# An eight-batch attention and feed-forward walk: the next batch's input norm made late in the walk, h in two halves, the cross-attention's exponential later

## The reference

```
x = x + cross_attention(layernorm(x), ctx)       # 16 heads of 64, 64 keys
n = layernorm(x)
dense:  q, k, v = n @ wq, n @ wk, n @ wv         # 16 heads of 16
        o = causal_softmax(q k / 4) v
        h = n + rmsnorm(o @ wo) * attn_norm_w
        d = h + rmsnorm(silu(h @ w1) * (h @ w3) @ w2) * ff_norm_w      # 1024 wide
sparse: top 2 of 8 experts by softmax(n @ router_w), each silu(n ew1) * (n ew3) @ ew2
        s = rmsnorm(weighted sum) * moe_norm_w
x = x + d + s
```

## Time and profile before

| | |
|---|---|
| median of 3 runs | 1732.98 us (1730.11 to 1733.04) |
| the profiled execution | 1727.69 us, its span 1725.6 us |
| mean granted clock of TensorE | 0.923 of full |
| busy PE, PEld, DVE, ACT, POOL | 83%, 55%, 48%, 32%, 31% |
| chain that ended last | PE 61%, DVE 13%, DMA 7%, POOL 6%, ACT 5%, SPq 4%, issue 4% |

### The profile page before, as it was taken

How to read it: one execution, slowest core, us unless ns; L and a number is a source line. 1 busy time by engine, 2 the same in 40 slices (tenths; PEclk the granted TensorE clock), 3 DMA queues, 4 the chain that set the end, 5 groups by cost and what they waited for, 6 DMA issues and landing times.

```text
span 1725.6 us, 23514 instructions
## 1 busy us (share of the span) xinstructions
PE 1435.5 (83%) x7689; PEld 945.7 (55%) x7690; DVE 834.7 (48%) x1733; ACT 551.2 (32%) x1178; POOL 533.1 (31%) x720
## 2 busy tenths in 40 slices
PE   7757998799879987998899879897988889999940
PEld 3533566556655665566556555664565365666620
DVE  0456435743664365446544644464347323333347
ACT  3230442154115402540343034304430513333322
POOL 3223215212422332233223331323142113555532
PEclk9985999999989998999899989998999889999975
DMA  5342007000600160025003400420050352222247
GB/s 216 126 101 59 2 4 156 14 1 19 141 14 1 37 123 14 1 64 97 13 1 89 72 13 1 115 45 14 1 123 13 44 156 65 88 85 85 85 165 255
DMA packets 107111, 117.18 MB, mean 68 GB/s; under 512 B 39416, under 2 KB 80912, under 8 KB 107024
## 3 DMA queue, kind: packets, MB, share of 16 engines
q1 hardware_dynamic: 88080, 98.10, 22.0%
q0 software_dynamic: 8576, 17.87, 3.3%
q10 hardware_dynamic: 10368, 0.04, 0.3%
HBM read 71.36 MB, written 44.21 MB: 67 GB/s over the span
## 4 chain that ended last, share of the span: by engine, by line
PE 61%; DVE 13%; DMA 7%; POOL 6%; ACT 5%; SPq 4%; issue 4%; ACTq 0%; POOLq 0%; DVEq 0%
PE ps L971 7%; PE ps L793 7%; PE ps L937 7%; PE ps L812 5%; DMA room<-parts_d 5%; DVE nm L1390 4%; PE ps L862 4%; PE ps L899 4%; PE ps L945 4%; PE ps L988 3%; PE ps L885 3%; SPq L501 3%; PE ps L826 2%; PE ps L782 2%; PE ps L919 2%
## 5 line engine op out<-in xcount | busy, mean ns | idle before, releaser
L1390 DVE TENSOR_REDUCE nm<-ps 128x2 f32<-128x256 f32 (+3 forms) x256 | 203.3, 821 | 139.2 <-PE ps L863 138.3
L1101 ACT ACTIVATE room<-ps 128x512 f32<-128x512 f32 x320 | 181.0, 598 | 152.4 <-PE ps L887 150.5
L937 PE MATMUL ps<-hT,w 128*128 128x512 f32 x768 | 213.5, 423 | 1.4 <-DVE hT L1418 1.4
L862 PE MATMUL ps<-room 96*128 96x128 bf16 (+3 forms) x512 | 135.5, 326 | 63.4 <-DMA room<-parts_d 43.3
L937 PEld LDWEIGHTS ps<-hT,w 128*128 128x128 f32 x768 | 145.3, 198 | 34.3 <-DVE hT L1418 3.3
L885 PE MATMUL ps<-room 99*128 99x384 bf16 (+3 forms) x512 | 132.2, 313 | 23.7 <-ACT room L1101 21.6
L1125 ACT ACTIVATE room<-ps 128x512 f32<-128x512 f32 x64 | 38.1, 596 | 343.3 <-PE ps L937 343.3
L971 PE MATMUL ps<-room 128*128 x288 | 137.4, 600 | 3.0 <-ACT room L1139 3.0
L945 PE MATMUL ps<-w,room 128*128 128x256 f32 x512 | 134.6, 393 | 0.0
L793 PE MATMUL ps<-room,xnT 128*128 128x512 f32 x256 | 133.0, 648 | 0.0
L1296 DVE TENSOR_TENSOR room<-ps,room 128x1024 f32<-128x1024 f32 x32 | 39.1, 1223 | 190.4 <-PE ps L793 190.4
(11 more groups left out here) (219 smaller groups left out, 2540.8 us busy)
## 6 DMA issues: line engine op xcount, KB each, us to landing
room<-parts_d SPq DMA_DIRECT2D x96, 256.0 KB, 6.7
room<-xs_d SPq DMA_DIRECT2D x72, 128.0 KB, 2.0
parts_d<-room SPq DMA_DIRECT2D x64, 128.0 KB, 1.8
room<-pair_d SPq DMA_DIRECT2D x8, 1024.0 KB, 7.7
room<-in_L_ffn_ew SPq DMA_DIRECT2D x24, 256.0 KB, 6.9
xin<-in_x SPq DMA_DIRECT2D x8, 512.0 KB, 11.8
parts_d<-xnT SPq DMA_DIRECT2D x32, 128.0 KB, 1.8
y_d<-hb SPq DMA_DIRECT2D x8, 512.0 KB, 2.6
```

The costliest lines, as they stand in the source:

```text
L862: mm(bank(o, n), q_rep[0:KREP, rep_at(h), t * P:n], k_rep[0:KREP, rep_at(h), 0:n], start=True, stop=False)
L937: last = mm(bank(up_banks(b, m)[i]), w[:, x, k, m * P:(m + 1) * P], hT[:, y, k, :], start=((x, y, k) == terms[0]), stop=((x, y, k) == term ...
L1101: done(fn(prob[:, u * 512:(u + 1) * 512], bank(6 + n % 2), ACT.Exp), "b_exp")
L1390: done(v.tensor_reduce(nm[:, t, 2 * hp:2 * hp + 2], pair_ps, AX.X, ALU.max, negate=True), "a_max")
```

## The change

- "x_stats" and "x_apply" leave `CROSS`; as "nx_stats" and "nx_apply" the same work is done for the next batch, behind "shift_parts" 0 in block 5 and at the end of block 6. Batch 0's stands at the head of walk 0, and walk 7 has none. POOL's root for it gets its own buffer and semaphore. "x_turn" comes after "m" 1 instead of after "m" 3 and "shift" 1.
- In the cross-attention "exp" 0 to 3 stand one or two PE steps later, and "sum" 1 between "cs" 2 0 and "cs" 2 1. PE's own order there stays as it was, but for "x_turn".
- "f_o_norm": POOL adds h in two halves of two tiles, each when its half of the scaled product is there; "f_h_turn" turns each half when it is ready.
- The net's first three blocks: gating on DVE ("fg" 0) comes before the second up product's step, and the routing steps and "slots" stand later.
- The maxima and sums of the cross-attention are counted by the general semaphore `dve_step`.
- The words of the change name replicating loads left with one queue; the kernel before has them all on SP's queue, and the diff touches no line of them.

```diff
 CROSS = [
-    ("x_stats",), ("m", 0), ("x_apply",), ("m", 1), ("m", 2), ("m", 3), ("shift", 1), ("x_turn",), ("bqk", 0), ("bqk", 1), ("f_hb",),
-    ("cs", 0, 0), ("cs", 0, 1), ("vw", 0), ("vw", 1), ("exp", 0), ("vw", 2), ("vw", 3), ("sum", 0), ("x_bias",),
-    ("cs", 1, 0), ("cs", 1, 1), ("exp", 1), ("sum", 1), ("ct", 0, 0), ("ct", 0, 1),
-    ("cs", 2, 0), ("cs", 2, 1), ("exp", 2), ("cv", 0, 0), ("cv", 0, 1), ("sum", 2), ("ct", 1, 0), ("ct", 1, 1),
-    ("cs", 3, 0), ("cs", 3, 1), ("exp", 3), ("cv", 1, 0), ("cv", 1, 1), ("sum", 3), ("ct", 2, 0), ("ct", 2, 1),
+    ("m", 0), ("m", 1), ("x_turn",), ("m", 2), ("m", 3), ("shift", 1), ("bqk", 0), ("bqk", 1), ("f_hb",),
+    ("cs", 0, 0), ("cs", 0, 1), ("vw", 0), ("vw", 1), ("vw", 2), ("exp", 0), ("vw", 3), ("sum", 0), ("x_bias",),
+    ("cs", 1, 0), ("cs", 1, 1), ("ct", 0, 0), ("ct", 0, 1), ("exp", 1),
+    ("cs", 2, 0), ("sum", 1), ("cs", 2, 1), ("cv", 0, 0), ("exp", 2), ("cv", 0, 1), ("sum", 2), ("ct", 1, 0), ("ct", 1, 1),
+    ("cs", 3, 0), ("cs", 3, 1), ("cv", 1, 0), ("exp", 3), ("cv", 1, 1), ("sum", 3), ("ct", 2, 0), ("ct", 2, 1),
...
-    ("v", 0), ("v", 1), ("f_h_turn",), ("v", 2), ("v", 3), ("route", 0), ("route", 1), ("fu", 0, 0), ("f_yb",), ("fu", 0, 1), ("fg", 0, 0), ("fg", 0, 1),
-    ("route", 2), ("fu", 1, 0), ("fu", 1, 1), ("fg", 1, 0), ("fg", 1, 1), ("fd", 0, 0), ("fd", 0, 1), ("slots",),
-    ("fu", 2, 0), ("fu", 2, 1), ("fg", 2, 0), ("fg", 2, 1), ("scatter",), ("fd", 1, 0), ("fd", 1, 1),
+    ("v", 0), ("v", 1), ("f_h_turn",), ("v", 2), ("v", 3), ("route", 0), ("fu", 0, 0), ("f_yb",), ("fg", 0, 0), ("fu", 0, 1), ("fg", 0, 1),
+    ("route", 1), ("fu", 1, 0), ("fg", 1, 0), ("fu", 1, 1), ("fg", 1, 1), ("route", 2), ("fd", 0, 0), ("fd", 0, 1),
+    ("fu", 2, 0), ("fg", 2, 0), ("fu", 2, 1), ("fg", 2, 1), ("slots",), ("scatter",), ("fd", 1, 0), ("fd", 1, 1),
...
-    STEPS += [("shift_parts", 0)] if _m == 5 else []
+    STEPS += {5: [("shift_parts", 0), ("nx_stats",)], 6: [("nx_apply",)]}.get(_m, [])
...
                     elif step[0] == "f_o_norm":
-                        need(pool, c, "wo_n", 2)
                         need(pool, c, "hb", 1)
-                        done(g.tensor_tensor(hb[:, :, :], hb[:, :, :], o_tok[:, :, :], ALU.add), "h")
+                        for i in range(2):
+                            need(pool, c, "wo_n", i + 1)
+                            done(g.tensor_tensor(hb[:, 2 * i:2 * i + 2, :], hb[:, 2 * i:2 * i + 2, :], o_tok[:, 2 * i:2 * i + 2, :], ALU.add), "h")
...
-                        turn(c, hb, (6, 7), lambda t2: [("h", 1)], "hT_ps")
+                        turn(c, hb, (6, 7), lambda t2: [("h", t2 + 1)], "hT_ps")
...
-                    if kind == "x_stats":
-                        need(dve, b, "x_in", 16)
+                    if kind in ("x_stats", "nx_stats"):
+                        n = b + (kind == "nx_stats")
+                        need(dve, n, "x_in", 16)
...
-                    elif kind == "x_apply":
-                        need(dve, b, "rstd1", 1)
+                    elif kind in ("x_apply", "nx_apply"):
+                        n = b + (kind == "nx_apply")
+                        need(dve, n, "rstd1", 1)
```

More of the change, by code:

```diff
@@ L125, in of_previous, with steps_of @@
     return step[0][0] == "f" or step[0] in OF_PREVIOUS or step == ("shift", 1)
-def steps_of(attention, net):
+def steps_of(attention, net, ahead=True):
     if attention:
-        return [s for s in STEPS if net or not of_previous(s)]
+        first = [] if net else [("x_stats",), ("x_apply",)]
+        return first + [s for s in STEPS if (net or not of_previous(s)) and (ahead or s[0][:2] != "nx")]
     order = [("shift", 1), ("f_hb",)] + SCORES + [("out_t", G - 1), ("f_o_turn",), ("f_wo",), ("f_wo_sq",), ("f_o_norm",), ("f_h_turn",), ("f_yb",)]
@@ L382, in walked @@
         def walked(b, c):
-            return steps_of(b is not None, c is not None)
+            return steps_of(b is not None, c is not None, b != B - 1)
         def in_tiles(eng, walk, peeled=1):
@@ L608, in batch @@
                 for step in walked(b, c):
-                    if step[0] == "x_stats":
-                        need(pool, b, "mv1", 1)
-                        rsqrt(b, rs1[:, :], mv1[:, :, 1], 0, "rstd1", "pool_a", ve_a)
+                    if step[0] in ("x_stats", "nx_stats"):
+                        n = b + (step[0] == "nx_stats")
+                        need(pool, n, "mv1", 1)
+                        done(g.tensor_tensor(ve_n[:, :], mv1[:, :, 1], eps[:, 0, :], ALU.add), "pool_n")
+                        need(pool, n, "pool_n", 1)
+                        done(g.tensor_tensor(rs1[:, :], ve_n[:, :], neg_half[:, :], ALU.pow), "rstd1")
                     elif step[0] == "x_turn":
@@ L1268, in batch @@
                     kind = step[0]
-                    if kind == "x_stats":
-                        need(dve, b, "x_in", 16)
+                    if kind in ("x_stats", "nx_stats"):
+                        n = b + (kind == "nx_stats")
+                        need(dve, n, "x_in", 16)
                         for t in range(T):
                             last = v.bn_stats(st1[:, t, :], xin[:, t, :])
-                        done(last, "stats")
-                        need(dve, b, "stats", 1)
+                        done(last, "stats1")
+                        need(dve, n, "stats1", 1)
                         carry_wait()
@@ L1297, in batch @@
                         need(dve, b, "sc_add", t + 1)
-                        done(v.tensor_reduce(cmax[:, t % 2, :], s3, AX.X, ALU.max), "sc_max")
-                        need(dve, b, "sc_max", t + 1)
+                        link(v.tensor_reduce(cmax[:, t % 2, :], s3, AX.X, ALU.max))
                         done(v.tensor_tensor(s3, s3, cmax[:, t % 2, :].unsqueeze(2).to_broadcast([P, CH, CK]), ALU.subtract), "sc_sub")
@@ L1306, in batch @@
                         s3 = s_sb[:, t % 2, :].rearrange("p (h k) -> p h k", h=CH)
-                        done(v.tensor_reduce(csum[:, t % 2, :], s3, AX.X, ALU.add), "sc_sum")
-                        need(dve, b, "sc_sum", t + 1)
+                        link(v.tensor_reduce(csum[:, t % 2, :], s3, AX.X, ALU.add))
                         done(v.reciprocal(crec[:, t % 2, :], csum[:, t % 2, :]), "sc_rec")
@@ L1316, in batch @@
                         done(v.bn_stats(st2[:, t, :], x1[:, t, :]), "stats")
-                        need(dve, b, "stats", 2 + t)
+                        need(dve, b, "stats", 1 + t)
                         carry_wait()
```

11 lines of the change are left out of this document (6 added, 5 removed).

## The result

The changed kernel takes **1682.44 us** (median of 4 runs, 1682.02 to 1683.12); the kernel before, 1731.55 in 4 runs beside it (1722.77 to 1733.04). The ratio is 0.9727 [0.9694, 0.976], so the change makes the kernel 2.7% faster. The forecast was 1690, the range 1662 to 1716. On the profiled executions the sum said -42.6, and 1727.69 became 1682.53: -45.2.

A forecast was written before the change was run, and what follows sets the result against it. PE's pauses were taken as the bound: replicating loads 43.3 us, normed input 42.9, score exponentials 21.6, sum h 15.2. Terms -29.4 - 25.2 - 3.5 + 16.2 + 0 + 0.8 - 1.5 = -42.6 from the 1733.0 median gave 1690, range 1662 to 1716.

The forecast's parts named there:

- 1. The boundary: Start of walks 2 to 7: without the norm, bias products start 4.9 us earlier, set by POOL's bias spread; -29.4 us.
- 2. The exponential: Cross-attention, walks 1 to 7: later exponentials remove PE's 2.42 us pause and slow products behind it; -3.6 a walk, -25.2 us.
- 3. Until the loads land: From q product to first row maximum: h halves and reordering gain nothing, swallowed by the replicating loads' wait; only scatter counted, -3.5.
- The scatter's term: Before the first row maximum: scatter starting 3 us later runs less beside the replicating loads; -0.5 a walk, -3.5 us.
- 4. The statistics: Late in walks 1 to 6: statistics delay mT's copy, +1.3 waiting and +1.4 lower clock a walk; +16.2 us.
- the term of +1.4 a walk: Behind PE's wait for mT in walks 1 to 6: the clock falls and slows products, +1.4 us a walk.
- 5. The application: Norm application late in the walk: fits DVE idling with POOL idle, avoiding about 1.7 us of blocking; 0, bounds 0 and +1.2.
- 6. The ends: Walk 0 with walk 1's beginning costs +0.8 us; the last walk gains about 1.5 from h in halves.
- A: Rival: neither the pause for mT nor that for the bias spread lowers the clock; saves 18.6 more, 1672; chance 0.25.
- B: Rival: the cross-attention's pause only moves a few products on, so the later exponential gives nothing; 1715; chance 0.15.
- C: Rival: the clock falls behind the late statistics and blocks 6 and 7 run at half; slower, 1772; chance 0.05.
- D: Rival: no effect, gains return as waits for replicating loads set by something other than the q product; about 1733; chance 0.05.

The follow-up runs named there:

- experiment 4: The changed kernel with routing, slots, gating and scatter put back in the order of the kernel before; 1738.11 us, ratio 0.9719 to the kernel before.
- the second profile of the kernel after: The changed kernel, unaltered, run again on another chip beside the kernel before; 1681.17 us, ratio 0.9717 to the kernel before.
- experiment 2: The kernel before with only the cross-attention's exponentials and sum 1 moved; 1702.17 us, ratio 0.9846 to the kernel before.
- experiment 1: The changed kernel with the cross-attention's exponentials and sum 1 put back; 1778.34 us, ratio 0.996 to the kernel before; second run 1779.89, 0.995.
- experiment 3: The changed kernel with exponentials' order, routing and h as in the kernel before, so the norm's move alone; 1765.04 us, ratio 0.988 to the kernel before.
- experiment 5: The changed kernel with h added in one piece again instead of two halves; 1755.94 us, ratio 0.9818 to the kernel before.
- experiment 7: The changed kernel with POOL's bias spread for the next batch moved into the walk before, ahead of y and z; 1723.85 us, ratio 0.964 to the kernel before.
- experiment 8: The changed kernel with the transposes of x put back behind m 3 and shift 1; 1742.26 us, ratio 0.9756 to the kernel before.
- experiment 6: The changed kernel with the next batch's statistics moved to the end of block 6 and their application to block 7; 1672.17 us, ratio 0.9674 to the kernel before.
- the first and the third group: Two of three groups of follow-up runs, each beside the kernel before; both on one chip, where the kernel before took 1783 us.

## Why the forecast held, step by step

*1. The boundary.* Right, with its mechanism: 12.7 us from m to the first score product was forecast, 12.7 is what walk 6 shows, the pause is 2.66 where I had 2.6, and POOL ends at the spread. PE waits 0.52 for the copy of m 1, where I had 0.8, which changes nothing. Walks 2 to 7 saved 32.1 where -29.4 stood: one of them kept its clock (1.6), and the stretches of before were up to 0.4 longer than walk 6's.

*2. The exponential.* Right in its mechanism, small by a fifth: -30.4 and not -25.2. The mis-sized term is the price of the pause. I took 2.4 for it and 1.2 for the four products at the low clock. The timelines give 2.42, then 1.30 for the four (3.23 and 1.93), and 0.27 for the small score products between the pause and them, from the first of which to the four it is 0.61 (1040.96 to 1041.57) and now 0.34 (1005.63 to 1005.97). Together 4.0 of the 4.3 a walk.

*3. Until the loads land.* The main claim, that what is won ahead of the q product is kept and h in halves is swallowed by the wait for the loads, stood up: PE's wait for h fell by 4.8 and the wait for the loads rose by 5.9. The scatter's term failed, -3.5 forecast where the stretch grew by 2.6, and its step was the guess that a scatter 3 us later leaves the loads alone. In walk 6 it moved from 24.1 to 26.7 us behind the q product, and experiment 4 shows no gain or loss by it. The +2.6 is no price of the change that could be named: the second profile of the kernel after has +1.6, and so has experiment 2, which touches nothing in that stretch.

*4. The statistics.* The wait is as forecast, +1.1 for +1.3. The clock is not: the term of +1.4 a walk was to be paid in six walks and came in one, walk 1 (its stretch is 47.4 here and 45.9 in the second profile of the kernel after, where the clock held in all six). That it fell so seldom is not safe to build on. On the other chip the same edit has the same wait of 1.72 to 1.73, and there the clock fell in or behind it in 22 walks of 42 (experiments 1, twice, 3, 4, 5, 7 and 8). The Trainium skill, "TensorE: Matmul & The Clock Gate", on loop structure, says that DVE copying a result out of PSUM "doesn't break PE warmth", that is, doesn't cost TensorE its clock. The walks of this kernel agree in five of six, those of the other chip in 20 of 42; and of the 1.73 only the last 0.38 is such a copy, the rest is mostly the statistics, so this is no clean case of that rule. What separates the two chips here is open; on the other one PE also has waits of up to 8 us in the disturbed stretch ahead of it.

The stretch grew by 10.5 against 16.2 forecast. The wait explains 6.8 of it; experiment 6 gives 6.3 back. The remaining 4 us, 0.6 a walk, can be the application, costed at nothing in part 5 and 1.38 long, but it was not isolated, and experiment 2 shows +1.8 in this stretch with nothing moved there.

*5. The application.* It takes 1.38 us with POOL idle, as in walk 0; the loss of 1.7 beside POOL is avoided. The prediction had the first of the four operations blocked. In walk 6 of the kernel before the trace has the first two at 1.25 us, each beside one of POOL's two copies of 1.03, and the last two at 0.40; the sum is the same.

*6. The ends.* Walk 0 is the term that was sized worst: +6.7, or 5.2 with the start and the beginning of walk 1, where +0.8 stood. Statistics and application on DVE go with the 1.6 behind its first maximum. Another 1.5 lies between the first m and the bias products, of which 1.3 came in experiment 2 as well. The largest piece, 3.2, is q to the first maximum, where the eight q products ran mostly at the low clock. PE's timeline of walk 0 in the kernel after:

```profile
105.68 6.42 PE L832 MATMUL ps<-xn2T,wq 128*128 128x512 f32 x8 [0.78 <-ACT xn2T L1046]
```

The pause ahead of them is 0.78 in both kernels, and they take 3.67 in the kernel before. Experiment 2, which leaves the norm alone, lost the same (31.6), and experiment 3, which is the norm move, did not (28.8). So it is no cost of the norm move; what decides it stays open. For the last walk -1.5 was forecast from h in halves; the part behind walk 7's first maximum is 0.7 shorter, and in experiment 2 it is 1.5 shorter without the halves.

**The rivals.** A (the clock holds; 1672) was half right: it held at the late statistics and fell at the boundary, each in five walks of six. B falls by experiments 1 and 2, each at 4.3 to 4.4 us a walk. C, slower by a clock at half over the last two blocks, falls by the windows behind the copy: at full in five walks, and in walk 1 back at full less than 5 us later. D falls with the table: the stretch with the wait for the loads took back 2.6 of 63.6.

The seven changes of the table make the 44.9 us by which the spans differ. That the forecast of -42.6 came so close is in part luck, for errors met: the gains of the exponential and the boundary were 5.2 and 2.7 larger than forecast and the loss by the statistics 5.7 smaller, against 6.1 more in the stretch before the loads land, 4.4 more in walk 0 and the beginning of walk 1, and 0.8 more at the end.

## What to carry to other kernels

When a late input is moved out of a boundary, write down the queue of the engine that is now last there: here POOL's y, z and spread set the new end to 0.06 us, and a copy of 1.03 us that needed neither of the two could go first for another 21 us. Where such a row sets the end of a boundary, slow products ahead of it cost nothing; once it is out of the way they do. Price a pause of TensorE with all that runs at the lower clock behind it, small products too. And place DVE work by who waits for DVE next: the same statistics cost 1.1 us a walk of waiting ahead of a copy that PE waits for, and one block later that wait is as short as it was before the change.

## What the runs showed that I had not expected

**The same pause, two clocks.** Behind the pause for the bias spread (2.64 to 2.67 us) the clock fell in five walks of six in the kernel after, in six of six in its second profile, and in 38 of 41 such pauses in the eight profiles that have them (the two of the kernel after, and experiments 1, twice, 3, 4, 5 and 6). Where m had run at the lower clock that pause was only 1.2 to 1.8 us, eight times with experiment 8, and the clock fell behind none of them. Behind 3.43 (experiment 8, five walks) it fell in three. Behind 2.41 in the cross-attention it fell in all seven walks of the kernel before and in 18 of 21 in experiments 1, twice, and 3; the three that kept it are their walks 1. Behind 1.72 ahead of m it fell in 14 walks of 66. A single walk says little of what a pause costs; at the low clock the boundary takes 1.1 to 1.6 us more.

**Chips differ in one stretch.** In the first and the third group, on one chip, DVE stood still in the middle of the first maxima, for instance in walk 5 of the second run of experiment 1:

```profile
998.83 0.42 DVE L1396 TENSOR_REDUCE nm<-ps 128x2 f32<-128x256 f32 x1 [5.14 <-remote]
1003.13 0.69 DVE L1396 TENSOR_REDUCE nm<-ps 128x2 f32<-128x512 f32 x1 [3.88 <-remote]
```

Over its span this makes, by the view of DVE's waits:

```profile
DVE nm L1396 <- remote: 58.3, 12, 8.8
```

The kernel after has no such wait in either of its two profiles. The stretch from the first maximum to the next m takes 55 us or so instead of 46. It holds for every kernel looked at there, while the boundary, the cross-attention and the stretch up to the first maximum agree with the other chip to 1 us a walk or better on average. The places lie beside the scatter and the loads of the next inputs. What DVE waits for there is not told by the profile, and was not tried.
